# Two quads of heads in the same strips of PSUM, and a new order of the steps in a slot, in a fused attention and mixture-of-experts layer

## The chip, the core and the metric

The kernel runs on one core of a Trainium2 chip. The metric is the device time of one execution, in microseconds (us). A core has TensorE (PE in the profile; its weight loads are PEld), VectorE (DVE), ScalarE (ACT), GpSimd (POOL) and SyncE (SP), which issues most DMAs. Each works through its own instructions in order, and they wait for one another on semaphores.

## What is computed

One transformer layer over x of 16 batches of 256 rows of 128 numbers, in float32: causal attention with 16 heads of 8 numbers, a projection, two layer norms, and for each row the two best of 14 experts (a 128x256 and a 256x128 layer with gelu), weighed, added and normed again. Cut to what matters:

```
qkv = target @ w_qkv;  q, k, v -> 16 heads of 8
scores = q k^T / sqrt(8), causal;  attn = softmax(scores)
out = attn @ v (heads side by side);  proj = out @ w_proj + b_proj
x = layernorm(target + layernorm(proj + target) * gamma + beta)
logits = x @ gate_w.T;  the two best experts of each row, their softmax weights
x = layernorm(x + clip(x + w0 * expert0(x) + w1 * expert1(x), -100, 100))
```

## The kernel before

There are three stages: attention with the choice of experts (until about 290 us in the profile), the expert tiles (to about 462 us), and the sums with the last layer norm. The change is in the first.

**Slots and units.** Each engine has a body(t, r, lap) that is run for t = 0 to B + 5 (B = 16 batches), unrolled. A slot t brings one new batch in and moves the others one step on: batch t is turned and projected to q, k, v; batch t-2 gets its row maxima; batches t-3 and t-4 their scores, exponentials and values; t-4 its projection, t-5 its norms and its gate, t-6 its row numbers and the scatter of its rows to DRAM. In a slot TensorE, ScalarE and GpSimd go through eight units u = 0 to 7. The order of the steps in the code is the order of the work.

**Row maxima.** maxima(t, r, i) on TensorE (L1485) fills both banks of M with q k^T of two or four pairs of heads, masked (L1506, L1512), for i = 0 to 5 at units 0 to 5. reduce(i) on VectorE (L1194, the instruction is L1202) takes the maxima. maxima(i) waits until reduce(i-1) is done, reduce(i) until maxima(i) are; there is one M. At u = 7 TensorE turns the row maxima (L1609), ScalarE negates them in two steps (L920, L931, with L1688 between), and a DMA puts them into q_stack.

**Scores and values.** scores (L1460) computes one pair of heads into S[n % 2], ScalarE takes the exponential (L862) into probs, and for four of the eight pairs GpSimd masks them (L748). values(t, r, s, k) (L1516) multiplies the four heads of quad k by probs. Each head has 32 columns of v_aug: 8 of values, a one (which gives the sum of the row), 23 zeros. So a head has a strip of 32 partitions of O, and a quad 128. Even quads go to columns 0 to 255 of O, odd ones to 256 to 511. pv_quad (L486) places quads 2 and 3 of batch t-4 at u = 2 and 3, quads 0 and 1 of batch t-3 at u = 5 and 7. ScalarE copies O (128x512) to heads_t at u = 7 (L938) and u = 3 (L896). turn_heads(t, i) (L1536) turns the four 128x128 blocks of one half of the rows into G at u = 4 and u = 5; VectorE divides them by the sums (invert_sums, L1211, and normalise_heads, L1217) into heads, which are turned again at u = 6 (L1712) and multiplied by wproj at u = 7 (L1681).

**What else stands in a slot of TensorE.** u = 1: the ranks (L1645) and the turn of x (L1550). u = 2: project (L1558). u = 4: the v projection into O (L1672), copied to v_aug by ScalarE (L899). u = 6: the turn of x2 (L1707), which waits for all six reductions, since it writes to M. u = 7: the gate (L1615), which waits for ScalarE's copy of that (x2T, L912). In each unit the order is: scores; at u = 7 the turn of the row maxima, then the gate; project; rank; turn of x; maxima; turn_heads(0) and the v projection; turn_heads(1); at u = 7 the projection of the heads and the second part of the shift; values; turn of x2 and of the heads.

**What else stands in a slot of VectorE.** From the first reduction on: means and variances (L1247), row_chosen (L1251), reduce(1), yg, row_no (L1234), reduce(2), ys, the split of q and k (rest, L1034), reduce(3), the statistics of ys, reduce(4), invert_sums(0), normalise_heads(0), reduce(5), the same for 1, then the search for the best experts (L1315, L1318), which waits for the gate, chosen (L1320), y (L1327), and the statistics of y (L1227). maxima(0) of the next slot wait for chosen, as its logits lie in M.

**GpSimd** issues the scatter of batch t-6 in four indirect DMAs (L775) at u = 2 to 5, once row_no is there.

## Time and profile before

| | us |
|---|---|
| median of 3 runs | 504.61 (498.4 to 506.06) |
| the profiled execution, its time | 504.69 |
| the profiled execution, its span | 502.9 |
| TensorE, VectorE busy | 379.2, 325.1 |
| ScalarE, GpSimd busy | 266.8, 290.3 |
| mean granted TensorE clock | 0.886 of 2.4 GHz |

The span goes from the first to the last instruction. The slots of the attention stage are counted from the first row-maximum reduction of one (reduce(0)) to that of the next. Slot 5 begins at 64.71 us, slot 7 at 95.82, slot 12 at 182.76, slot 13 at 198.93, slot 16 at 251.68. "remote" in a row means that the profile didn't tell whose signal ended the wait.

### The profile page before, as it was taken

How to read it: one execution, taken by the hardware profiler on the slowest of the kernel's cores; microseconds unless marked ns; L12 is line 12 of the kernel's file. 1: busy time of each engine (PE TensorE's matmuls, PEld its weight loads, DVE VectorE, ACT ScalarE, POOL GpSimd, SP SyncE). 2: the span in 40 equal slices, each digit the busy share in tenths (PEclk: the TensorE clock that was granted, in tenths of full speed). 3: DMA queues.
4: the chain of work that ended last, by engine and by line, in shares of the span. 5: the costliest groups of instructions: out<-in, count | busy, mean ns of one | idle time of the engine just before them, and what ended most of it. 6: DMA issues, size and time to landing. Idle time of an engine off the chain costs nothing. (4 is left out here: it accounts for less than half of the span.)

```text
span 502.9 us, 12961 instructions
## 1 busy us (share of the span) xinstructions
PE 379.2 (75%) x4207; PEld 276.0 (55%) x4207; DVE 325.1 (65%) x1053; ACT 266.8 (53%) x624; POOL 290.3 (58%) x454
## 2 busy tenths in 40 slices
PE   5477988977988798879877867765577877777780
PEld 3244555655555555556544435765466867756580
DVE  6634687758777877786786846734444776663386
ACT  2124666756776577666645637443346544444054
POOL 6402346775777668666754365785554555556271
PEclk9556999989999899998989869978787989798996
DMA  5412333334334433442311141222332222220573
GB/s 137 106 52 65 85 101 98 103 87 110 101 91 107 110 84 90 118 113 66 89 50 55 42 68 28 64 69 63 94 108 67 70 69 75 71 69 21 169 230 105
DMA packets 72974, 44.02 MB, mean 88 GB/s; under 512 B 13233, under 2 KB 68931, under 8 KB 72796
## 3 DMA queue, kind: packets, MB, share of 16 engines
q1 hardware_dynamic: 66650, 33.11, 25.0%
q0 software_dynamic: 4640, 9.36, 5.7%
q10 hardware_dynamic: 1618, 0.73, 0.6%
q8 instruction: 34, 0.56, 0.5%
q14 instruction: 32, 0.26, 0.2%
HBM read 18.54 MB, written 12.36 MB: 61 GB/s over the span
## 5 line engine op out<-in xcount | busy, mean ns | idle before, releaser
L1202 DVE TENSOR_REDUCE row_max<-M 128x4 f32<-128x1024 f32 (+1 forms) x96 | 117.2, 1221 | 48.8 <-PE M L1512 37.3
L862 ACT ACTIVATE probs<-S 128x768 f32<-128x768 f32 x128 | 102.7, 816 | 58.3 <-PE S L1481 42.5
L729 POOL DMA_INDIRECT results<-tile_rows x77 | 77.2, 1002 | 57.0 <-DVE tile_rows L1074 37.4
L775 POOL DMA_INDIRECT sorted_rows<-x,row_no x64 | 65.7, 1027 | 33.5 <-DVE row_no L1234 21.0
L1506 PE MATMUL M<-k_stack,q_stack 64*128 64x128 bf16 (+1 forms) x512 | 41.7, 267 | 43.4 <-DVE row_max L1202 40.3
L1531 PE MATMUL O<-probs,diag 128*32 128x256 f32 (+1 forms) x1024 | 58.5, 349 | 3.1 <-DVE row_chosen L1251 3.1
L748 POOL TENSOR_SCALAR_AFFINE_SELECT probs<-probs 128x256 f32<-128x256 f32 x104 | 40.0, 409 | 23.3 <-ACT probs L862 23.2
L1506 PEld LDWEIGHTS M<-k_stack,q_stack 64*128 64x128 bf16 x512 | 16.7, 100 | 62.6 <-DVE row_max L1202 57.0
L1473 PE MATMUL S<-q_stack,k_stack 64*128 64x256 bf16 (+1 forms) x512 | 45.6, 260 | 0.0
L1531 PEld LDWEIGHTS O<-probs,diag 128*32 128x32 f32 x1024 | 27.7, 113 | 25.4 <-issue 9.3
L852 ACT ACTIVATE hT<-S,q_stack 128x128 f32<-128x128 f32 x78 | 25.7, 371 | 25.0 <-PE S L1577 16.0
L782 POOL TENSOR_TENSOR diag<-rest,diag 128x512 bf16<-128x512 f32 x16 | 18.5, 1155 | 35.5 <-ACT diag L882 24.7
L852 ACT ACTIVATE hT<-S,k_stack 128x128 f32<-128x128 f32 x76 | 24.8, 371 | 20.5 <-PE S L1577 9.7
L1577 PE MATMUL S<-rows_t,k_stack 128*128 128x128 f32 x152 | 28.3, 318 | 7.7 <-ACT hT L852 4.4
L1512 PE MATMUL M<-ident_fold,mask_m 64*128 64x128 bf16 (+1 forms) x384 | 33.1, 255 | 0.0
L1577 PE MATMUL S<-rows_t,q_stack 128*128 128x128 f32 x156 | 27.1, 301 | 4.4 <-issue 2.7
L1577 PEld LDWEIGHTS S<-rows_t,k_stack 128*128 128x128 f32 x152 | 24.7, 231 | 8.9 <-issue 8.9
L1584 PE MATMUL M<-k_stack,hT 128*128 128x128 f32 x132 | 24.5, 317 | 4.1 <-DVE tile_rows L1074 3.5
L1473 PEld LDWEIGHTS S<-q_stack,k_stack 64*128 64x128 bf16 x512 | 16.6, 97 | 19.4 <-issue 17.1
L1065 DVE COPY q_stack<-experts 128x642 f32 x39 | 21.7, 559 | 8.0 <-issue 5.0
L1577 PEld LDWEIGHTS S<-rows_t,q_stack 128*128 128x128 f32 x156 | 23.4, 215 | 5.4 <-issue 5.3
L1584 PE MATMUL M<-q_stack,hT 128*128 128x128 f32 x116 | 21.9, 319 | 5.1 <-DVE tile_rows L1074 5.0
(261 smaller groups left out, 861.5 us busy)
## 6 DMA issues: line engine op xcount, KB each, us to landing
q_stack<-diag SPq DMA_DIRECT2D x96, 64.0 KB
k_stack<-diag SPq DMA_DIRECT2D x85, 64.0 KB
tile_rows<-sorted_rows SPq DMA_DIRECT2D x77, 64.5 KB
experts<-in_L_ffn_w_dram SPq DMA_DIRECT2D x28, 128.0 KB
xin<-in_L_attn_target_dram SPq DMA_DIRECT2D x16, 128.0 KB, 3.0
xres<-in_L_attn_target_dram SPq DMA_DIRECT2D x16, 128.0 KB, 3.1
out_dram<-probs SPq DMA_DIRECT2D x8, 256.0 KB, 2.3
q_stack<-results SPq DMA_DIRECT2D x7, 256.0 KB, 3.2
```

Source lines behind the costliest of these rows:

```text
L729: pool.indirect_dma_start(results, bass.IndirectOffsetOnAxis(ap=y_rows[:, slot, D:ROW].bitcast(U32), axis=0), y_rows[:, slot, 0:D], None, ...
L748: last = pool.affine_select(out=diag, in_=diag, compare_op=ALU.is_ge, fill=0.0, base=0, pattern=[[0, 2], [1, P]], channel_multiplier=-1)
L775: pool.indirect_dma_start(sorted_rows, bass.IndirectOffsetOnAxis(ap=row_no[:, q * 2 * TT + n:q * 2 * TT + n + 1], axis=0), x2[:, q, n % 2, ...
L852: act.activation(hT[:, (s - 2) % HR, f], hidden_of(s - 2, f), ACT.Gelu, bias=expert_now[(s - 2) % XR][:, AT_B1 + f:AT_B1 + f + 1]).then_in ...
L862: act.activation(probs[:, n].rearrange("p (a q) -> p a q", a=2), S[n % 2][:, :].rearrange("p (a q) -> p a q", a=2)[:, :, 0:T + P], ACT.Exp ...
L1202: dve.tensor_reduce(row_max[:, (r - 2) % R, :, g0:g0 + ng, half], M_both[:, :].rearrange("p (a h k) -> p a h k", a=2, h=ng), X, ALU.max).t ...
L1473: last = pe.matmul(S[n % 2][:, 512 * a + at:512 * a + at + nq], k_stack[rows, b, n, half * P:half * P + P], q_stack[rows, b, n, T - nq:T], ...
L1506: pe.matmul(M[a][:, j * keys:j * keys + keys], q_stack[rows, b, g0 + j, half * P:half * P + P], k_stack[rows, b, g0 + j, 0:keys], start=(j ...
L1512: last = pe.matmul(diag, mask_m[rows, c], ident_fold[rows, None, :].broadcast_to([TILE, ng, TILE]), start=False, stop=(c == 1), skip_group ...
L1531: last = pe.matmul(O[32 * j:32 * j + 32, at + T - nq:at + T], v_aug[:, b, half, h], probs[:, h // 2, (h % 2) * (T + P) + of:(h % 2) * (T + ...
L1577: pe.matmul(hidden_of(s - 2, f), expert_now[(s - 2) % XR][:, f * P:f * P + P], rows_t[:, (s - 2) % HR], start=True, stop=True).then_inc(h_ ...
L1584: last = pe.matmul(second(s - 4), hT[:, (s - 4) % HR, f], expert_now[(s - 4) % XR][:, AT_W2 + f * D:AT_W2 + f * D + D], start=(f == 0), st ...
```

## The change

Storage: the four heads of a quad now lie in 4 x 32 columns followed by 16 columns of zeros (v_quads, 144 columns a quad). An odd quad is read 16 columns further left, so its values and sums come out on partitions 16 to 31 of each strip and zeros on 0 to 15. Both quads of a pair are added up in the same 256 columns of O: the even one starts the sum, the odd one ends it. So the copies of O are 128x256, heads_t has two blocks instead of four, turn_heads makes two transposes instead of four, and the heads come out in another order. w_proj's rows are put in that order once, by a matmul with a reordered identity at t = 1, with two copies on VectorE for the identity and one for the result. GpSimd clears the 16 columns in one more memset.

Order on TensorE: maxima stand last in their unit (behind turn_heads, the v projection and values), values stand behind turn_heads(1) and, at u = 7, behind the turn of the row maxima and ahead of the gate, the projection and the second part of the shift. On VectorE invert_sums(0) and normalise_heads(0) stand ahead of reduce(4), and those of 1 ahead of reduce(5).

```diff
+        QUADS = H // 4
+        VQ = 4 * 32 + 16
+        V_SIZE = R * TT * QUADS * VQ
+        v_quads = v_flat.rearrange("p (n c) -> p n c", c=VQ)
+        v_heads = v_quads[:, :, 0:4 * 32].rearrange("p n (j c) -> p n j c", j=4)
...
-        heads_t = sb("heads_t", [P, 4, T])
+        heads_t = sb("heads_t", [P, 2, T])
...
-            sp.dma_start(wproj[:, :], w_proj).then_inc(weights_in, 16)
+            sp.dma_start(wproj_raw, w_proj).then_inc(weights_in, 16)
...
+                pool.memset(v_quads[:, :, 4 * 32:VQ], 0.0).then_inc(consts_p, 1)
...
-                        act.copy(heads_t[:, 2:4], O[:, :].rearrange("p (k q) -> p k q", k=2)).then_inc(o_copied, 1)
+                        act.copy(heads_t[:, 1], O[:, 0:T]).then_inc(o_copied, 1)
...
-                        act.copy(heads_t[:, 0:2], O[:, :].rearrange("p (k q) -> p k q", k=2)).then_inc(o_copied, 1)
+                        act.copy(heads_t[:, 0], O[:, 0:T]).then_inc(o_copied, 1)
...
+            def order_ident():
+                dve.wait_ge(consts, 3)
+                for a in range(2):
+                    part = slice(TILE * a, TILE * a + TILE)
+                    dve.tensor_copy(ident_order[:, part].rearrange("p (j b d) -> p b j d", j=4, b=2),
+                                    ident[:, part].rearrange("p (b j d) -> p b j d", j=4, b=2)).then_inc(ordered, 1)
...
                 dve.wait_ge(gate_turned, 1)
+                dve.tensor_copy(wproj[:, :], M[0][:, P:P + D])
...
-                reduce(4)
                 if on(t - 4):
                     invert_sums(0)
                 if on(t - 4):
                     normalise_heads(0)
+                reduce(4)
                 steps(t, 4)
-                reduce(5)
                 if on(t - 4):
                     invert_sums(1)
                 if on(t - 4):
                     normalise_heads(1)
+                reduce(5)
...
-                at = (k % 2) * T
                 for half, of, nq in ((0, 0, T), (1, T, P)):
                     for j in range(4):
                         h = 4 * k + j
-                        last = pe.matmul(O[32 * j:32 * j + 32, at + T - nq:at + T], v_aug[:, b, half, h],
+                        at = ((b * TT + half) * QUADS + k) * VQ + 32 * j - 16 * (k % 2)
+                        last = pe.matmul(O[32 * j:32 * j + 32, T - nq:T], v_flat[:, at:at + 32],
                                          probs[:, h // 2, (h % 2) * (T + P) + of:(h % 2) * (T + P) + of + nq],
-                                         start=(half == 0), stop=(half == 1), skip_group_check=True)
+                                         start=(half == 0 and k % 2 == 0), stop=(half == 1 and k % 2 == 1), skip_group_check=True)
...
-                for k in range(4):
+                for k in range(2):
                     last = pe.transpose(G[:, k * P:k * P + P], heads_t[:, k, i * P:i * P + P], ident[:, :])
...
+                            pe.wait_ge(ordered, 2)
+                            pe.matmul(M[0][:, P:P + D], ident_order, wproj_raw, start=True, stop=True).then_inc(gate_turned, 1)
...
-                    if u < NM and on(t - 2):
-                        maxima(t, r, u)
...
                     if u == 5 and on(t - 4):
                         pe.wait_ge(o_normed, 2 * (t - 4) + 1)
                         turn_heads(t, 1)
+                    if pv_quad(t, u) and on(pv_quad(t, u)[0]):
...
+                        values(t, r, *pv_quad(t, u))
+                    if u == 7 and on(t - 5):
+                        pe.wait_ge(x2T_copied, t - 4)
...
-                    if pv_quad(t, u) and on(pv_quad(t, u)[0]):
...
-                        values(t, r, *pv_quad(t, u))
...
                         last.then_inc(on_turned, 1)
+                    if u < NM and on(t - 2):
+                        maxima(t, r, u)
```

## Rows read from the trace of the kernel before

**Rows 1.** the page, part 1: each engine, busy us (share of the span), instructions.

```profile
PE 379.2 (75%) x4207; PEld 276.0 (55%) x4207; DVE 325.1 (65%) x1053; ACT 266.8 (53%) x624; POOL 290.3 (58%) x454
```

**Rows 2.** windows (slots, one stretch): PE, PEld, DVE, ACT, POOL busy; PEclk, DMA share, GB/s.

```profile
95.82:114.45 18.63, 15.50 (x213) 10.16 (x211) 12.76 (x35) 11.39 (x24) 12.43 (x23) 0.91 0.33 91
101.30:104.70 3.40, 1.25 (x28) 0.68 (x24) 1.71 (x3) 2.23 (x4) 2.23 (x3) 1.00 0.54 143
164.55:182.76 18.21, 15.50 (x213) 10.17 (x211) 12.76 (x35) 11.53 (x24) 12.27 (x23) 0.91 0.34 94
182.76:198.93 16.17, 14.01 (x213) 9.07 (x210) 12.64 (x36) 11.40 (x24) 11.71 (x21) 1.00 0.39 105
198.93:215.83 16.90, 13.99 (x213) 9.04 (x209) 12.64 (x36) 11.39 (x24) 12.15 (x23) 1.00 0.37 102
215.83:235.33 19.50, 16.68 (x213) 10.80 (x209) 12.75 (x36) 11.48 (x24) 12.60 (x24) 0.82 0.33 88
```

**Rows 3.** the view by lines, VectorE, 95.82 to 251.68 us: xcount | busy, mean ns | idle before.

```profile
L1202 DVE TENSOR_REDUCE row_max<-M 128x4 f32<-128x1024 f32 (+1 forms) x54 | 66.0, 1222 | 21.5 <-PE M L1512 10.6 <-remote 8.4 <-issue 1.3
...
L1315 DVE MAX8 top_v_all<-M 128x8 f32<-128x14 f32 x18 | 2.3, 171 | 16.7 <-PE M L1615 16.7
```

**Rows 4.** the timeline of VectorE, slots 5, 12, 13: start us, us, instruction, [idle before <-releaser].

```profile
70.75 1.21 DVE L1202 TENSOR_REDUCE row_max<-M 128x4 f32<-128x1024 f32 x1
...
189.57 1.23 DVE L1202 TENSOR_REDUCE row_max<-M 128x4 f32<-128x1024 f32 x1 [0.69 <-PE M L1512]
...
198.93 1.22 DVE L1202 TENSOR_REDUCE row_max<-M 128x4 f32<-128x1024 f32 x1 [0.24 <-PE M L1512]
...
200.75 1.23 DVE L1202 TENSOR_REDUCE row_max<-M 128x4 f32<-128x1024 f32 x1 [0.24 <-PE M L1512]
...
202.69 1.22 DVE L1202 TENSOR_REDUCE row_max<-M 128x8 f32<-128x1024 f32 x1
...
206.47 1.23 DVE L1202 TENSOR_REDUCE row_max<-M 128x4 f32<-128x1024 f32 x1 [1.43 <-remote]
...
208.38 1.19 DVE L1202 TENSOR_REDUCE row_max<-M 128x4 f32<-128x1024 f32 x1
209.49 0.25 DVE L1211 RECIPROCAL inv_sum<-G 128x16 f32<-128x16 f32 x1
209.77 0.29 DVE L1217 TENSOR_TENSOR heads<-G,inv_sum 128x128 f32<-128x128 f32 x1
210.29 1.23 DVE L1202 TENSOR_REDUCE row_max<-M 128x8 f32<-128x1024 f32 x1 [0.23 <-PE M L1512]
...
213.71 0.26 DVE L1315 MAX8 top_v_all<-M 128x8 f32<-128x14 f32 x2 [1.71 <-PE M L1615]
...
215.83 1.22 DVE L1202 TENSOR_REDUCE row_max<-M 128x4 f32<-128x1024 f32 x1 [0.24 <-PE M L1512]
```

**Rows 5.** the timeline of TensorE, the slot at 198.93 us.

```profile
202.58 0.86 PE L1531 MATMUL O<-probs,diag 128*32 128x256 f32 x16
203.37 0.34 PE L1473 MATMUL S<-q_stack,k_stack 64*128 64x256 bf16 x4
...
204.41 0.86 PE L1531 MATMUL O<-probs,diag 128*32 128x256 f32 x16
...
207.75 0.39 PE L1506 MATMUL M<-k_stack,q_stack 64*128 64x256 bf16 x4 [2.10 <-DVE row_max L1202]
...
208.18 0.66 PE L1539 MATMUL G<-ident,heads_t 128*128 128x128 f32 x4
...
211.82 0.44 PE L1707 MATMUL M<-ident,x 128*128 128x128 f32 x2
```

**Rows 6.** the timelines of ScalarE and GpSimd, same slot.

```profile
206.63 0.59 ACT L896 COPY heads_t<-O 128x512 f32<-128x512 f32 x1 [0.94 <-PE O L1531]
...
209.32 0.37 ACT L899 COPY diag<-O 128x256 f32<-128x256 f32 x1 [1.40 <-PE O L1672]
...
204.83 0.96 POOL L775 DMA_INDIRECT sorted_rows<-x,row_no  x1 [0.30 <-issue]
```

More of the change, by code:

```diff
@@ L170, in transformer_layer @@
         yg = sb("yg", [P, TT, D])
+        wproj_raw, ident_order = yg[:, 0], yg[:, 1]
         ys = sb("ys", [P, TT, D])
@@ L300, in transformer_layer @@
         folded = sem("folded")
+        ordered = sem("ordered")
         consts_v = sem("consts_v")
@@ L484, in s_unit, with values_of @@
             return (t - 3, u - 2) if u >= 2 else (t - 4, u + NP - 2)
+        def values_of(r):
+            return v_heads[:, r * TT * QUADS:(r + 1) * TT * QUADS, :, 0:HD]
         def pv_quad(t, u):
@@ L707, in more_constants @@
             def more_constants():
-                pool.memset(v_aug[:, :, :, :, HD:32], 0.0).then_inc(consts_p, 1)
+                pool.memset(v_heads[:, :, :, HD:32], 0.0).then_inc(consts_p, 1)
+                pool.memset(v_quads[:, :, 4 * 32:VQ], 0.0).then_inc(consts_p, 1)
                 pool.wait_ge(consts_p, 1)
-                pool.memset(v_aug[:, :, :, :, HD:HD + 1], 1.0).then_inc(consts_p, 1)
+                pool.memset(v_heads[:, :, :, HD:HD + 1], 1.0).then_inc(consts_p, 1)
                 pool.memset(earlier[:, :], 1.0).then_inc(iotas, 1)
@@ L895, in body @@
                         after(act, o_turned, 2 * (t - 4))
-                        act.copy(heads_t[:, 2:4], O[:, :].rearrange("p (k q) -> p k q", k=2)).then_inc(o_copied, 1)
+                        act.copy(heads_t[:, 1], O[:, 0:T]).then_inc(o_copied, 1)
                     if u == 4 and on(t) and not early(t):
                         act.wait_ge(v_ready, t + 1)
-                        act.copy(v_aug[:, r, :, :, 0:HD],
-                                 O[:, 0:T].rearrange("p (i h d) -> p i h d", i=TT, h=H)).then_inc(v_copied, 1)
+                        act.copy(values_of(r), O[:, 0:T].rearrange("p (n j d) -> p n j d", j=4, d=HD)).then_inc(v_copied, 1)
                     if u == 5 and on(t - 5):
@@ L1183, in body @@
                     keep_values(t, r)
+                    order_ident()
                     numbers()
@@ L1611, in body @@
                         last.then_inc(shift_turned, 1)
-                    if u == 7 and on(t - 5):
-                        pe.wait_ge(x2T_copied, t - 4)
-                        for i in range(TT):
-                            last = pe.matmul(M[0][:, T + i * E:T + i * E + E], x2T[:, (r - 5) % R, i * P:i * P + P], gate_t[:, :],
-                                             start=True, stop=True)
-                        last.then_inc(gate_ready, 1)
                     if u == 0 and t == 0:
@@ L1677, in body @@
                         turn_heads(t, 1)
+                    if pv_quad(t, u) and on(pv_quad(t, u)[0]):
+                        if u == 2 and on(t - 6):
+                            pe.wait_ge(rank_read, t - 5)
+                            if t == B + 1:
+                                pe.wait_ge(first_table, 1)
+                        if u == 5 and on(t):
+                            pe.wait_ge(v_copied, t + 1)
+                        values(t, r, *pv_quad(t, u))
+                    if u == 7 and on(t - 5):
+                        pe.wait_ge(x2T_copied, t - 4)
+                        for i in range(TT):
+                            last = pe.matmul(M[0][:, T + i * E:T + i * E + E], x2T[:, (r - 5) % R, i * P:i * P + P], gate_t[:, :],
+                                             start=True, stop=True)
+                        last.then_inc(gate_ready, 1)
                     if u == 7 and on(t - 4):
```

29 lines of the change are left out of this document (11 added, 18 removed).

## The prediction, made before the changed kernel ran

> **What bounds the kernel now.** First the page's line of busy times, then stretches by window, then one slot's timelines on VectorE, TensorE, ScalarE and GpSimd. On the page TensorE has the largest share, 75% of 502.9 us [rows 1], but that is an average over stages. The change acts in the attention stage, whose period is the slot t: sixteen batches go through it, one new per slot, each slot with eight units u. So I read one slot and ask what ends each wait.
>
> VectorE has 12.64 us of work in a slot of 16.17 us and in one of 16.90 us, TensorE 14.0 us [rows 2]. Grouped by line over nine slots (95.82 to 251.68 us), VectorE stands idle 21.5 us ahead of the six row-maximum reductions a slot and 16.7 us ahead of the top-8 search (L1315) that waits for the gate [rows 3]: 2.4 and 1.9 us a slot, and close to nothing elsewhere. So VectorE sets the slot, together with those TensorE steps that it waits for. Both engines share one buffer M: maxima(i) can't begin before reduce(i-1) has ended, and reduce(i) not before maxima(i).
>
> In the slot that starts at 198.93 us the six reductions start at 198.93, 200.75, 202.69, 206.47, 208.38 and 210.29, the search at 213.71, and the next slot's first reduction at 215.83 [rows 4]. The fourth waits 1.43 us, though its maxima were issued before 204.41, where the values behind them start [rows 4, 5]. Their signal arrives late, and so does that of these values: they end at 205.27 by their row, and ScalarE's copy of O (L896), which waits for them, starts at 206.63 [rows 5, 6]. Meanwhile GpSimd issues its scatter of rows twice, close together, the second from 204.83 to 205.79 [rows 6]. The slots before the first scatter don't have this wait: the fourth reduction of slot 5, at 70.75 us, stands without one [rows 4]. I call it the held signal and take its place as tied to the scatters, which hang on the second reduction of the slot; nothing in the change moves them against that.
>
> TensorE's own largest wait in the slot is 2.10 us ahead of maxima(4) at 207.75, for reduce(3) [rows 5].
>
> **The clock.** Three slots are longer than their neighbours: 18.63, 18.21 and 19.50 us, at a mean granted clock of 0.91, 0.91 and 0.82, against 16.17 and 16.90 at 1.00 (mean 16.54) [rows 2]. Together that is 56.34 - 3 x 16.54 = 6.7 us. Ahead of the first of them, in 101.3 to 104.7 us, TensorE was busy 1.25 of 3.40 us, the hold and the wait for reduce(3) in one piece [rows 2]; then it was granted half its clock (1.2 instead of 2.4 GHz).
>
> **The change, part by part**, in the slot at 198.93.
>
> (a) At u = 2 values(t-4,2) now stand ahead of maxima(2). By start to start the values take 203.37 - 202.58 = 0.79 us [rows 5]. VectorE is ready for reduce(2) at 202.69 and had it at once; now maxima(2) end 0.79 later and reduce(2) starts 0.8 us later. VectorE's work behind it (ys, rest) moves along. Bounds: +0.8 if nothing covers it, 0 if TensorE had room, which it hasn't: project ends as maxima(2) begin.
>
> (b) At u = 3 values(t-4,3) stand ahead of maxima(3). VectorE is now ready for reduce(3) 0.8 us later, 205.85 instead of 205.04, but the held signal comes at 206.4 all the same. So 1.43 us of cover hides the 0.8 of (a): net 0 at reduce(3). In two or three slots the wait was shorter (0.69 us at 189.57 [rows 4]) and some of (a) shows: 0.5 us over all. Without a scatter (slots 4, 5) there is no cover, and in slot 6 nearly none: 3 x 0.8 = 2.4 us.
>
> (c) At u = 4 the order on VectorE is now reciprocal and scaling of the first half of the heads, then reduce(4). Between reduce(3) and reduce(4) come 0.28 + 0.29 = 0.57 us (starts at 209.49 and 209.77, 0.29 long [rows 4]). TensorE is ready: turn_heads(0) (0.66 us long with its four transposes [rows 5]) and the v projection, of as many matmuls of that width, now run while reduce(3) runs, as soon as ScalarE has copied O at 206.63 + 0.37 = 207.0, and are done near 208.0. A group of maxima takes 0.6 us from the end of one reduction (200.15) to the start of the next (200.75 [rows 4]), so maxima(4) end near 208.6, before VectorE asks at 208.95. The four transposes of a turn become two, so half of the 0.66, some 0.3 us, goes each time, unseen. reduce(4) comes 1.91 + 0.54 = 2.45 us after reduce(3). Price +0.54; if VectorE were not the bound here it would be between -0.2 and +0.54.
>
> (d) At u = 5 turn_heads(1) and values(t-3,0) (0.79) stand ahead of maxima(5). They fit under reduce(4), which takes 1.2 us; then maxima(5) need 0.6 us and VectorE does its other 0.57 meanwhile. reduce(5) again comes 1.9 us after reduce(4): 0.
>
> (e) From reduce(5) to the search. Before: it ends at 211.51, the turn of x2 (L1707) comes at 211.82, behind values and scores, then scores and the turn of the row maxima, the gate (L1615), and the search at 213.71 [rows 4, 5]. x2 waits for all reductions, so now it starts 0.05 us after the last: -0.26. Then the same steps up to the turn of the row maxima, and there values(t-3,1) come ahead of the gate: +0.79. ScalarE's copy of x2T stands beside these steps before and after, so it gives nothing back. Net +0.53. VectorE has nothing else to do: it waits 2.7 us for the gate instead of 1.71 [rows 4]. Bounds: 0 (if the gate's place were free) and +0.79.
>
> (f) From the search to the next reduce(0): 2.12 us before, of which VectorE works until 215.59 and waits 0.24 for maxima [rows 4]. Now TensorE has less behind the gate and VectorE is the bound: 1.90 us, so -0.22. maxima(0) must also wait for the chosen experts, which come in the middle of this work; by my sum VectorE remains the bound by 0.1.
>
> (g) Less work: the two copies of O have half the elements. They took 0.59 us; a copy of that half size, L899, 0.37 [rows 6]. 0.4 us a slot on ScalarE, 0.6 on TensorE in the transposes. In slots 4 to 17 neither sets the time. In the two slots behind, where no maxima are left and TensorE and ScalarE pace the chain, I take -0.3 each.
>
> (h) Once, at the start: two small copies for the reordered identity, one matmul and one copy for the reordered projection weights, a second memset on GpSimd. Each is no larger than the 0.37 us copy [rows 6] but the memset, which nothing waits for until slot 3. Between 0 (beside other work) and 4 x 0.37 = 1.5 us; I take 0.3, since this stage waits for its loads. The queue of SP gets the same DMAs.
>
> **Sum.** An ordinary slot: 0.54 + 0.53 - 0.22 = +0.85 us. Slots 5 to 17 are thirteen: 11.1. Uncovered (a): 2.4 + 0.5 = 2.9. Together +14.0. Less 0.6 in the tail, plus 0.3 at the start: +13.7. Against it stands the clock: TensorE now works through the hold (turn_heads(0) and v from 207.0), its longest wait falls from 2.1 to about 1.3 us, and the three falls of the clock in this stage should mostly go. I take back 6 of the 6.7 us. Result +7.7 us. The profiled execution took 504.69 us (span 502.9, 1.8 around it), as good as the median of 504.61: 504.7 + 7.7 = 512.4, **512 us**.
>
> A rule of the Trainium skill bears on (b). "SBUF - State Buffer", Who interferes with whom, says that a DMA never contends with a compute engine and that TensorE's ports wait on nobody. By that rule the hold would not come from the scatters and would be part of TensorE's own order; what that gives is the second rival below. The rows speak against the rule only by coincidence in time. On the clock, "TensorE: Matmul & The Clock Gate", Part 1, says that idle stretches bring the half-rate state and sustained work ends it; the rows agree (1.25 busy of 3.40 us ahead of the fall), and it is why I expect some of the falls to go.
>
> **Rivals.**
> 1. *TensorE, not VectorE, is the bound, and in-order waits were its cost: faster.* Place: maxima(4) no longer stop the head's turn and the v projection behind them (2.10 us of waiting, rows 5), and maxima(2), (3), (5) no longer stop values. From the point where reduce(2) starts no later than 1.94 us after reduce(1), each slot gets shorter by what TensorE no longer waits, some 2.10 - 1.3 = 0.8 us, and 0.6 for the transposes that go: at the best 13 x 1.4 = 18, 487 us. VectorE has 12.64 of work in a slot of 16.5 and waits elsewhere, so I halve that: 504.7 - 9 = 496, and with the falls of the clock gone 490. For it: TensorE's 75% share and 14.0 busy us. Against: VectorE waits for the gate already, and the gate moves back.
> 2. *The hold belongs to TensorE's order.* Then it moves back with maxima(3), (a) is covered nowhere, and nine slots pay 0.8 more: +7.2, 520 us.
> 3. *The falls of the clock stay.* 512 + 6 = 518 us. For it: TensorE still waits in this stage, at other places.
> 4. *The gate's place costs nothing*, since ScalarE's copy held it anyway: without (e) 13 x 0.53 = 6.9 less, 505 us, no change.
>
> **Chances.** Forecast 0.42, its own range 507 to 517; rival 1 0.20; rival 2 0.13; rival 3 0.10; rival 4 0.15. The range 494 to 520 leaves out the better half of rival 1 and the top of 2 and 3. A measurement of this kernel can tell about 2% from no change (494.5 and 514.7 us): faster by over 2% 0.18, within 0.50, slower 0.32.
>
> **What would show it.** Right: search 3.95 us behind reduce(5) (3.42 before) with an idle time of 2.7; reduce(2) 2.75 us behind reduce(1); reduce(3) still 7.5 us behind reduce(0); reduce(4) 2.45 behind reduce(3); slots of 17.0 to 17.8 us; clock near 1.00 through 64 to 250 us. Wrong: an idle time ahead of the search near 1.7 (rival 4), a fourth reduction 8.3 us behind the first (rival 2), slots under 16 us (rival 1).

## The result, and the profile after: slower by 5%

The changed kernel took 531.11 us (median of 4 runs, 525.61 to 541.79), the kernel before 504.13 us on the same chip: ratio 1.0536, 95% interval 1.0414 to 1.0657. The forecast of 512 us missed, and so did its range. The ratio leaves out slow executions, that of 541.79 us among them, and the profile of the kernel before is of an execution of 504.69 us, 1.3% above its fastest. The profiled execution took 525.61 us, 20.9 more than that of before.

The page of the changed kernel: part 1, and from part 5 the row-maximum reductions (L1225, before L1202) and the search (L1338, before L1315).

```profile
PE 376.8 (72%) x4145; PEld 276.7 (53%) x4145; DVE 323.0 (62%) x1056; ACT 262.3 (50%) x624; POOL 290.4 (55%) x455
...
L1225 DVE TENSOR_REDUCE row_max<-M 128x4 f32<-128x1024 f32 (+1 forms) x96 | 117.3, 1222 | 58.8 <-PE M L1535 57.5
...
L1338 DVE MAX8 top_v_all<-M 128x8 f32<-128x14 f32 x32 | 4.1, 170 | 45.4 <-PE M L1708 41.8
```

No engine is busy more than 0.7 us longer than before [rows 1]; the time went into waits. The view by lines over the same nine slots as in [rows 3] (7 to 15, now 97.28 to 268.14 us: 170.9 us instead of 155.9) says where:

```profile
L1225 DVE TENSOR_REDUCE row_max<-M 128x4 f32<-128x1024 f32 (+1 forms) x54 | 65.9, 1220 | 29.3 <-PE M L1535 28.2 <-remote 1.0
...
L1338 DVE MAX8 top_v_all<-M 128x8 f32<-128x14 f32 x18 | 2.3, 170 | 24.5 <-PE M L1708 24.5
```

The reductions wait 29.3 us (21.5 before), the search 24.5 (16.7 before): +15.6 in nine slots. The rest of the 20.9: slots 5, 6 and 16 are 1.4, 3.2 and 3.1 us longer, the start 3.2 shorter (reduce(0) of slot 5 at 61.53 us, 64.71 before), and some 1.5 come behind slot 16.

Windows of the changed kernel: the stage, slot 13, the 3.41 us at half clock in it (last row) and as long a stretch ahead of that (columns as in [rows 2]).

```profile
64.00:276.00 212.00, 164.62 (x2301) 107.98 (x2299) 141.75 (x396) 125.32 (x245) 131.37 (x241) 0.90 0.32 88
209.93:228.55 18.62, 14.53 (x210) 9.73 (x205) 12.62 (x36) 11.28 (x24) 12.09 (x22) 0.91 0.34 92
214.75:218.16 3.41, 1.65 (x34) 1.02 (x27) 2.53 (x5) 1.98 (x4) 2.32 (x3) 1.00 0.53 142
218.16:221.57 3.41, 3.41 (x28) 2.20 (x31) 3.17 (x9) 1.86 (x4) 1.98 (x6) 0.50 0.40 101
```

Such a fall now comes in every slot from 6 on, nine between 64 and 250 us, where the kernel before had three stretches at half clock; so has pack_alone below, which keeps that order. The timeline of VectorE in slot 13, reductions and search:

```profile
209.93 1.21 DVE L1225 TENSOR_REDUCE row_max<-M 128x4 f32<-128x1024 f32 x1
...
211.75 1.22 DVE L1225 TENSOR_REDUCE row_max<-M 128x4 f32<-128x1024 f32 x1 [0.25 <-PE M L1535]
...
214.42 1.22 DVE L1225 TENSOR_REDUCE row_max<-M 128x8 f32<-128x1024 f32 x1 [0.81 <-PE M L1535]
...
217.65 1.22 DVE L1225 TENSOR_REDUCE row_max<-M 128x4 f32<-128x1024 f32 x1 [0.88 <-PE M L1535]
...
220.18 1.23 DVE L1225 TENSOR_REDUCE row_max<-M 128x4 f32<-128x1024 f32 x1
...
222.97 1.22 DVE L1225 TENSOR_REDUCE row_max<-M 128x8 f32<-128x1024 f32 x1 [1.08 <-PE M L1535]
226.77 0.26 DVE L1338 MAX8 top_v_all<-M 128x8 f32<-128x14 f32 x2 [2.58 <-PE M L1708]
...
228.55 1.21 DVE L1225 TENSOR_REDUCE row_max<-M 128x4 f32<-128x1024 f32 x1
```

Against [rows 4], step by step: reduce(2) 2.67 us behind reduce(1) (1.94 before), reduce(3) 7.72 behind reduce(0) (7.54), reduce(4) 2.53 (1.91), **reduce(5) 2.79 (1.91)**, search 3.80 (3.42), next reduce(0) 1.78 (2.12). The slot is 18.62 us; eight of the nine take 18.6 to 19.0, slot 15 takes 20.95. The timeline of TensorE shows why reduce(5) is late here:

```profile
216.20 0.28 PE L1504 MATMUL S<-ident_fold,mask_s 64*128 64x128 bf16 x4
217.98 0.55 PE L1562 MATMUL G<-ident,heads_t 128*128 128x128 f32 x2 [1.50 <-ACT heads_t L911]
218.32 1.06 PE L1689 MATMUL O<-wqk_raw,flat 128*128 128x128 f32 x4
...
221.00 1.11 PE L1554 MATMUL O<-probs,flat 128*32 128x256 f32 x16
222.05 0.40 PE L1529 MATMUL M<-k_stack,q_stack 64*128 64x128 bf16 x8
222.28 0.38 PE L1535 MATMUL M<-ident_fold,mask_m 64*128 64x256 bf16 x4
```

TensorE waits 1.50 us for ScalarE's copy of the heads, its clock falls at 218.16, and the v projection (1.06 us; 0.61 at full clock) and the values (1.11; 0.86) push maxima(5) to 222.66. GpSimd issues three of its four scatters between 214 and 222 us:

```profile
214.43 1.09 POOL L790 DMA_INDIRECT sorted_rows<-x,row_no  x1 [1.68 <-DVE row_no L1257]
215.82 0.96 POOL L790 DMA_INDIRECT sorted_rows<-x,row_no  x1 [0.30 <-issue]
...
221.50 1.07 POOL L790 DMA_INDIRECT sorted_rows<-x,row_no  x1 [0.17 <-issue]
```

Which part of the late reduce(5) is TensorE's own, the signals tell. In slots 6, 8, 10, 12 and 14 reduce(5) starts 0.04 us behind the end of maxima(5), so all of the 3.2 to 3.3 us from reduce(4) is TensorE's late work. In slots 7, 9, 11 and 13 it starts 0.3 us behind that end, in slots 15 and 16 1.1 and 0.9: there the signal itself is late too, and the scatter of step 4 (221.50 in slot 13) starts 0.4 to 1.2 us ahead of the end of maxima(5).

### The profile page after: what moved, and what is told of

Same layout as the page of the kernel before. It is cut to its first block and busy times, and to the rows that moved or that the text cites. A ratio compares the mean times of both kernels' runs of the same rounds, so it can differ in the third digit from the quotient of the medians.

```text
span 523.9 us, 12841 instructions
## 1 busy us (share of the span) xinstructions
PE 376.8 (72%) x4145; PEld 276.7 (53%) x4145; DVE 323.0 (62%) x1056; ACT 262.3 (50%) x624; POOL 290.4 (55%) x455
## 5 line engine op out<-in xcount | busy, mean ns | idle before, releaser
L1225 DVE TENSOR_REDUCE row_max<-M 128x4 f32<-128x1024 f32 (+1 forms) x96 | 117.3, 1222 | 58.8 <-PE M L1535 57.5
L1554 PE MATMUL O<-probs,flat 128*32 128x256 f32 (+1 forms) x1024 | 66.7, 372 | 3.0 <-DVE row_chosen L1274 3.0
L1554 PEld LDWEIGHTS O<-probs,flat 128*32 128x32 f32 x1024 | 32.7, 120 | 28.4 <-issue 15.0
L797 POOL TENSOR_TENSOR flat<-rest,flat 128x512 bf16<-128x512 f32 x16 | 18.5, 1154 | 42.2 <-ACT flat L897 24.8
L1562 PE MATMUL G<-ident,heads_t 128*128 128x128 f32 x64 | 17.0, 355 | 22.5 <-ACT heads_t L911 14.3
L1338 DVE MAX8 top_v_all<-M 128x8 f32<-128x14 f32 x32 | 4.1, 170 | 45.4 <-PE M L1708 41.8
L1600 PE MATMUL S<-rows_t,k_stack 128*128 128x128 f32 x152 | 26.8, 304 | 6.5 <-ACT rows_t L861 4.5
L1600 PE MATMUL S<-rows_t,q_stack 128*128 128x128 f32 x156 | 28.5, 313 | 3.7 <-issue 1.8
L1600 PEld LDWEIGHTS S<-rows_t,k_stack 128*128 128x128 f32 x152 | 23.1, 217 | 7.5 <-issue 7.5
L1600 PEld LDWEIGHTS S<-rows_t,q_stack 128*128 128x128 f32 x156 | 24.7, 226 | 4.3 <-issue 4.3
L1607 PEld LDWEIGHTS M<-k_stack,hT 128*128 128x128 f32 x132 | 19.7, 215 | 11.7 <-issue 11.4
```

What stands on the lines that cost most here:

```text
L1225: dve.tensor_reduce(row_max[:, (r - 2) % R, :, g0:g0 + ng, half], M_both[:, :].rearrange("p (a h k) -> p a h k", a=2, h=ng), X, ALU.max).t ...
L1554: last = pe.matmul(O[32 * j:32 * j + 32, T - nq:T], v_flat[:, at:at + 32], probs[:, h // 2, (h % 2) * (T + P) + of:(h % 2) * (T + P) + of ...
L1600: pe.matmul(hidden_of(s - 2, f), expert_now[(s - 2) % XR][:, f * P:f * P + P], rows_t[:, (s - 2) % HR], start=True, stop=True).then_inc(h_ ...
L1607: last = pe.matmul(second(s - 4), hT[:, (s - 4) % HR, f], expert_now[(s - 4) % XR][:, AT_W2 + f * D:AT_W2 + f * D + D], start=(f == 0), st ...
```

## The experiments

All were timed against the kernel before on the same chip; times of different sessions are compared by their ratios. Theory 1 at first: the new order makes TensorE wait in one piece, and its clock falls behind that wait. Its rival: VectorE's own waits are enough. Theory 1 had a second part, from the prediction: TensorE's signals are held back where two scatters stand close together.

**Parts of the change, scatters as they were.** a_warm gives TensorE work in the wait, with two extra 256-column matmuls into G whose result nothing reads:

```diff
                     if u == 4 and on(t - 4) and on(t):
+                        pe.wait_ge(rest_left, t + 1)
+                        for i in range(2):
+                            pe.matmul(G[:, 0:T], ident[:, :], xT[:, r], start=True, stop=True)
```

> The changed kernel with two added float32 matmuls of 128x256 into G at u = 4 (identity by xT), between the split of q and k and the first turn of the heads, in slots 4 to 15; their result is overwritten. They fill a wait of TensorE of 1.5 us with about 1.1 us of work. Theory 1 (the fall of the clock in every slot is a large part of the loss): the falls of the clock between 100 and 250 us become fewer, reduce(5) comes about 1.9 us behind reduce(4) instead of 2.8 to 3.3, slots of about 17.6 us instead of 18.8, in all 8 to 12 us less than the changed kernel (about 519). Theory 2 (the order alone costs it, the clock is a by-product): the same time as the changed kernel within 3 us, or longer by the added work.

Measured: 536.92 us, 1.0762 (1.066 to 1.0863). Six half-clock stretches between 64 and 250 us instead of nine, but longer ones, a mean clock there of 0.89 instead of 0.92, and slots of 20.0 to 20.8 us. Filling that wait did not help; the stretches came elsewhere. It is no clean test, since the added matmuls (1.13 us at full clock) also stand ahead of maxima(4).

a_gate_first puts only the values of step 7 back behind the gate's scores, the projection and the shift:

```diff
-                    if pv_quad(t, u) and on(pv_quad(t, u)[0]):
+                    if u != 7 and pv_quad(t, u) and on(pv_quad(t, u)[0]):
...
                                   start=False, stop=True, skip_group_check=True).then_inc(shift_left, 1)
+                    if u == 7 and on(t - 3):
+                        values(t, r, t - 3, 1)
```

> The changed kernel with one step put back: at u = 7 values(t-3,1) stand behind the gate, the projection and the second part of the shift again. By my step (e) the search then comes 3.1 us behind reduce(5) instead of 3.8, its idle time is 1.8 instead of 2.6, and the piece from the search to reduce(0) is about 2.1 instead of 1.8: 0.4 to 0.5 us a slot less, 5 to 7 us in all. If TensorE's row of work and not VectorE's wait for the gate set the slot, nothing changes within 2 us.

Measured: 529.26 us, 1.0636 (1.0536 to 1.0735). In slot 7 the search stands 3.15 us behind reduce(5) and waits 1.93, so the gate's place costs 0.65 us. The 5 to 7 us in all did not come: in slots 6 and 7 it is given back at half clock, with 3.3 to 3.8 us from the search to the next reduce(0), and in slots 6, 8, 11 and 14 the search itself stands 4.3 to 4.4 us behind reduce(5).

pack_alone keeps the packing and the new numbering of the values, with the order of before on both engines:

```diff
+                    if u < NM and on(t - 2):
+                        maxima(t, r, u)
                     if u == 4 and on(t - 4):
                         pe.wait_ge(o_copied, 2 * (t - 3))
```

> The packing of two quads into the same strips alone: the storage, the smaller copies and the two transposes of the change, with the order of the kernel before on TensorE and VectorE. By my step (g) these save work that sets no time: 504 us within 4. If the packing itself costs something (the odd read, the accumulation over two quads), it comes out slower than 508.

Measured: 502.31 us, 1.0111 (0.9987 to 1.0235): no difference that can be told. The loss is the order's.

a_max_first puts all maxima and VectorE's order back and leaves the values' new place; a_max23_first puts back only maxima(2) and (3):

```diff
+                    if u in (2, 3) and on(t - 2):
+                        maxima(t, r, u)
                     if u == 4 and on(t - 4):
...
-                    if u < NM and on(t - 2):
+                    if u < NM and u not in (2, 3) and on(t - 2):
                         maxima(t, r, u)
```

> The changed kernel with the maxima put back ahead of the slot's other work at every step, and VectorE's order put back with them; the values stay where the change put them, behind the turn of the row maxima. Theory 1 (it is the maxima's place that costs, by the waits of VectorE and by the clock): reduce(2) and reduce(4) come 1.9 us behind the one ahead again, the half-clock stretch is not in every slot, only the search stands 3.8 instead of 3.4 us behind reduce(5), and the time is 504 to 510, some 22 to 26 us less than after. Rival (it is the values' place): 522 or more.

Measured: 509.33 us, 1.0065 (1.0021 to 1.0109), within the 504 to 510 of theory 1. So most of the loss lies in the maxima's place. Seven falls are left between 64 and 250 us, in slot 7 and in slots 9 to 14.

> The changed kernel with maxima(2) and maxima(3) alone put back ahead of the slot's other work. Theory 1 (the fall of the clock in each slot follows TensorE's wait of 1.5 us ahead of the turn of the heads, which the late signal of values(3) sets, so these maxima do not touch it): reduce(2) 1.9 us behind reduce(1), reduce(3) held until the same moment, the falls stay in every slot, 527 to 532. Rival (the work of steps 2 and 3, done too early or too late, decides whether the clock falls): falls in less than half of the slots, 510 to 518.

Measured: 529.38 us, 1.0523 (1.0448 to 1.0598). So putting maxima(2) and (3) back gains nothing while the signals are held; the late maxima(4) and (5) stay suspected.

**The scatters a step later.** The four scatters of a slot stood at steps 2 to 5; here they stand at 3 to 6, in the changed kernel (a_scatter_later), in the kernel before (b_scatter_later) and with the packing alone (pack_later). The edit, against the changed kernel:

```diff
-            return {3: (0,), 4: (1,), 5: (2,), 6: (3,)}.get(u, ()) if t >= B + 4 else {2: (0,), 3: (1,), 4: (2,), 5: (3,)}.get(u, ())
+            return {3: (0,), 4: (1,), 5: (2,), 6: (3,)}.get(u, ())
```

> The changed kernel with the four scatters of rows one unit later (u = 3 to 6) in all slots, so that GpSimd has the subtraction for the split (L797) and the norm's small steps between the first and the second. If the held signals belong to two scatters close together, reduce(3) no longer waits 0.85 us, TensorE's wait ahead of the turn of the heads gets shorter, the clock falls less often: 10 us less or more (near 515). If the hold belongs to TensorE's order, the fourth reduction still waits 0.85 us, and the time is that of the changed kernel, or longer, since GpSimd is later.

Measured: 512.88 us, 1.0319 (1.0211 to 1.0428), near the 515 that was expected if the held signals belong to the scatters.

> The kernel before, with the four scatters of a slot at steps 3, 4, 5, 6 in every slot instead of at 2, 3, 4, 5 (the last stage does so already). Theory 1 (TensorE's signals are held back while two scatters stand close together, in both orders alike): reduce(3) no longer waits (idle before it 0.5 to 1.7 us before, then near 0), so a slot of full clock takes 15.3 to 15.8 us, and the time falls by 6 to 12 us, to 490 to 496. Rival (the 18 us that later scatters gave the changed kernel came from its order of TensorE's work only): within 2 us of the kernel before.

Measured: 485.15 us, 0.9626 (0.9571 to 0.9681), with no fall of the clock between 64 and 250 us.

> The packing of two quads in the same strips with the order of before on both engines, and the scatters at steps 3 to 6. Theory 1: the two are independent and each engine keeps the order of before, so 488 to 496, faster than both kernels. Rival (packing shortens TensorE's work, and with the hold gone too its clock falls more often): reduce(5) waits 1 us and more in most slots as in the changed kernel, and the time is 500 to 510.

Measured: 485.16 us, 0.961 (0.954 to 0.9681). Both came out below what was expected. Reduce(3) waits 0.08 us at most in slots 6 to 15 of either. So the hold is tied to the scatters, in either order, and a kernel 3.8% faster than before lies one step of the scatters away. The window 64 to 250 us shows the clock, in b_scatter_later:

```profile
64.00:250.00 186.00, 163.34 (x2435) 105.19 (x2435) 148.38 (x408) 128.68 (x250) 135.28 (x249) 1.00 0.39 101
```

The same window of pack_later:

```profile
64.00:250.00 186.00, 160.82 (x2393) 100.58 (x2394) 148.35 (x410) 127.26 (x254) 137.70 (x252) 1.00 0.38 102
```

And of the changed kernel:

```profile
64.00:250.00 186.00, 144.75 (x2034) 95.28 (x2032) 125.86 (x350) 112.94 (x221) 117.11 (x217) 0.92 0.34 91
```

**Which part of the order, with the scatters at 3 to 6.** Same edits as above on a_scatter_later: all maxima first (a_maxfirst_later), maxima(4) and (5) first with VectorE's order back (a_max45_later), maxima(2) and (3) first (a_max23_later). Maxima(0) and (1) stay late in the last two. b_first_alone is the kernel before with its scatters at 2, 4, 5, 6.

> The changed kernel with its scatters at steps 3 to 6, all maxima back ahead of the slot's other work and VectorE's order back; of the new order only the values' place is left. Theory 1 (the values' place costs what it adds ahead of the gate's scores, 0.4 us of waiting before the search less 0.2 to 0.3 us behind it): reduce(5) to the search 3.8 to 4.0 us, no fall of the clock between 64 and 250 us, 487 to 491. Rival (the values' place brings falls by itself, as it had some in nearly every slot while the signals were held): 500 or more.

Measured: 482.88 us, 0.970 (0.957 to 0.9831); one fall, at 240 us.

> The changed kernel with its scatters at steps 3 to 6, maxima(4) and maxima(5) and VectorE's order back, maxima(0) to maxima(3) behind the slot's other work. Theory 1 (the late reduce(2) makes ScalarE's middle part of the split late, the copy of the heads stands behind that on ScalarE, and the turn of the heads makes TensorE wait 1.26 us in one piece, behind which its clock falls): that wait stays, falls stay in at least half of the slots, 500 to 509. Rival (only the sum of VectorE's waits counts, 0.73 us of step 2 and 0.3 us at the search): few falls, 493 to 498.

Measured: 496.81 us, 0.9939 (0.9895 to 0.9983): the rival. From slot 6 to 12 no fall, though TensorE waits as long as ever, now ahead of maxima(4):

```profile
169.79 0.39 PE L1528 MATMUL M<-k_stack,q_stack 64*128 64x256 bf16 x4 [1.47 <-DVE row_max L1224]
```

> The changed kernel with its scatters at steps 3 to 6 and maxima(2) and maxima(3) back ahead of the slot's other work; maxima(4) and maxima(5) stay late, with VectorE's new order. Theory 1: TensorE's wait of 1.26 us ahead of the turn of the heads is gone, falls in at most a quarter of the slots, 0.54 us more of VectorE's time between reduce(3) and reduce(4) and 0.3 us at the search, so 492 to 498. Rival (the late maxima(4) and maxima(5) bring the falls): reduce(5) 2.7 us and more behind reduce(4) in most slots, 504 to 513.

Measured: 507.87 us, 1.0244 (1.0064 to 1.0424): the rival again, and three stretches at half clock between 64 and 250 us. Theory 1 had picked the wrong maxima, and the length of TensorE's one wait as the sign.

> The kernel before with its first scatter at step 2 as it was and the other three at steps 4, 5, 6, so that the first two no longer stand 1.4 us apart. Theory 1 (it takes two scatters close together to hold TensorE's signals back): no wait before reduce(3), 483 to 489, like the kernel with all four a step later. Rival (a scatter at step 2 holds them, whether another follows or not): reduce(3) waits 0.5 to 1.7 us as before, 498 to 506.

Measured: 481.31 us, 0.9659 (0.9476 to 0.9842). Reduce(3) waits 0.03 us at most in slots 7 to 15. The second part of theory 1 had expected that, but it doesn't show that two scatters are needed. In slots 7 to 9 maxima(3) are due 1.04 us behind the one scatter at step 2, and their signal comes 0.34 to 0.54 us late all the same, just in time for VectorE.

**What holds the signal.** The second part of theory 1, two scatters close together, was wrong as well, and a_scatter_later shows it in two slots at full clock. The timeline of GpSimd in slots 9 and 10, the scatter of step 4:

```profile
144.41 1.07 POOL L789 DMA_INDIRECT sorted_rows<-x,row_no  x1 [0.17 <-issue]
...
162.31 1.07 POOL L789 DMA_INDIRECT sorted_rows<-x,row_no  x1 [0.17 <-issue]
```

The timeline of TensorE in the same slots, the end of maxima(5):

```profile
144.50 0.38 PE L1534 MATMUL M<-ident_fold,mask_m 64*128 64x256 bf16 x4
...
162.16 0.38 PE L1534 MATMUL M<-ident_fold,mask_m 64*128 64x256 bf16 x4
```

The timeline of VectorE, reduce(5), which waits for them:

```profile
145.72 1.23 DVE L1224 TENSOR_REDUCE row_max<-M 128x8 f32<-128x1024 f32 x1 [1.03 <-PE M L1534]
...
162.58 1.23 DVE L1224 TENSOR_REDUCE row_max<-M 128x8 f32<-128x1024 f32 x1 [0.23 <-issue]
```

Maxima(5) end 0.47 us behind the scatter's start in slot 9, and reduce(5) starts 0.84 us after that; in slot 10 they end 0.23 us behind it, and reduce(5) starts 0.04 us later. One scatter is enough. A signal is due at the end of the work that sends it. Of the TensorE signals due 0.4 to 1.2 us behind the start of a scatter, 32 of 44 came late in this kernel (80 to 262 us), most of them 1.26 to 1.66 us behind that start; in the changed kernel 25 of 29, those behind the second of two close scatters up to 2.06 us. Of VectorE's and ScalarE's own signals due in the same stretches of the two kernels, none of 69 came even 0.1 us late. Theory 2 is this: each scatter holds back the TensorE signals that are due soon behind its start. The two bounds are those of the count: in the changed kernel maxima(3) are due 0.38 us behind the second scatter and are held too. With the scatters at 3 to 6 it is the scatter of step 4 that catches maxima(5), in ten of the eleven slots 6 to 16; maxima(4) and (5) put first end before it. In b_scatter_later 51 of 56 such signals are late too, but no reduction waits for one directly; the cost is in which signal a scatter catches. It isn't nothing there either: in seven of the nine slots 7 to 15 reduce(2) waits 0.5 us, behind a chain that starts with a held signal. The timeline of all engines in slot 13 of b_scatter_later has it:

```profile
189.10 0.98 POOL L774 DMA_INDIRECT sorted_rows<-x,row_no  x1 [0.17 <-issue]
...
190.71 0.81 ACT L861 ACTIVATE probs<-S 128x768 f32<-128x768 f32 x1 [0.66 <-PE S L1480]
...
191.84 1.13 PE L1557 MATMUL G<-diag,wqk 128*128 128x256 f32 x4 [0.44 <-ACT diag L866]
...
193.56 1.23 DVE L1201 TENSOR_REDUCE row_max<-M 128x8 f32<-128x1024 f32 x1 [0.53 <-PE M L1511]
```

The scores are due at 189.57, 0.47 us behind the scatter, and ScalarE starts on them at 190.71 only. Its copy of the turned x comes behind that, the projection waits 0.44 us for the copy, and maxima(2) come behind the projection.

Theory 2 asked for the scatters at 3, 5, 6, 7 (a_scatter_3567), and for the copy of the heads ahead of the cast on ScalarE, which should take TensorE's wait ahead of the turn away (a_scatter_copy, with the scatters at 3, 5, 6, 7: the block of `heads_t[:, 1]` moved above that of `part_m`). a_max45_first is the changed kernel with maxima(4) and (5) alone put back, scatters as they were.

```diff
-            return {3: (0,), 4: (1,), 5: (2,), 6: (3,)}.get(u, ())
+            return {3: (0,), 5: (1,), 6: (2,), 7: (3,)}.get(u, ())
```

> The changed kernel with its scatters at steps 3, 5, 6, 7. With them at 3 to 6 the scatter of step 4 began 0.46 us ahead of the end of maxima(5), and their signal came 0.8 to 1.1 us late. Theory 2 (each scatter holds back the TensorE signals that fall due 0.4 to 1.3 us behind its start, until 1.3 to 1.7 us behind it): reduce(5) comes 1.9 us behind reduce(4) wherever the clock is full, slots of 16.7 to 16.9 us, and 494 to 501. Rival (the wait before reduce(5) comes from the late maxima and the clock, not from a scatter): reduce(5) 2.7 us and more behind reduce(4) in most slots, 508 to 514.

Measured: 459.94 us, 1.0248 (1.0196 to 1.0301). Reduce(5) comes 1.94 us behind reduce(4) and a slot takes 16.7 us, as theory 2 had it; but this chip took only 448.5 us for the kernel before, and its trace shows few late signals, so that is no test of the theory.

> The one before this (the changed kernel, scatters at 3, 5, 6, 7) with ScalarE's copy of the heads at step 3 ahead of its middle part of the split. If TensorE's wait of 1.26 us ahead of the turn of the heads brings falls of the clock: that wait shrinks below 0.6 us, the falls between 64 and 250 us get fewer, and the time is 4 us or more below the one before this. Rival (this wait lies on no path and brings no falls): within 3 us of it.

Measured: 461.58 us, 1.0272 (1.0226 to 1.0318). The wait is 0.43 us instead of 1.26 and the time is the same; but the run above has no fall to take away, so whether the wait brings falls it can't tell.

> The changed kernel, scatters where they were, with maxima(4) and maxima(5) alone put back ahead of the slot's other work and VectorE's order with them. Theory 2 (most of the loss comes from the late maxima(4) and maxima(5): 0.5 us ahead of reduce(4), and 1 us and more ahead of reduce(5)): reduce(4) and reduce(5) come 1.9 us behind the one ahead in most slots, 508 to 514. Rival (the late maxima(2), through ScalarE's late copy of the heads, brings the falls of the clock): 523 to 530.

Measured: 465.62 us, 1.0363 (1.0293 to 1.0433): neither expectation fits in us, on a chip 55 us quicker. As a ratio the rival's does (523 of 504.1 is 1.037), but there are no held signals here for either to be about. So three kernels ran on one chip once more; it was again one of the quick kind (448.75 us for the kernel before).

> The changed kernel, unaltered, on one chip with the two after it. The chip of the last three ran the kernel before in 448.5 us and showed no held signal of TensorE behind a scatter. Theory 2 (held signals and the falls of the clock that come with them make the loss beyond the sum of 0.85 us in a slot): on a chip with held signals 1.05 to 1.06 of before; on a chip without them reduce(3) waits 0 and reduce(5) comes 1.9 us behind reduce(4), and 1.02 to 1.03 of before. Rival (the order alone brings the loss): 1.05 or more on either.

Measured, the changed kernel unaltered: 463.83 us, **1.0326** (1.0258 to 1.0394), next to the 1.02 to 1.03 that theory 2 had for such a chip. The rival, 1.05 or more by the order alone, is refuted.

> The changed kernel with its scatters at steps 3, 5, 6, 7 once more, since the first chip it ran on showed no held signals and could not tell. On a chip that shows them, theory 2: reduce(5) 1.9 us behind reduce(4) where the clock is full, and 0.985 to 1.005 of before, against 1.03 with them at 3, 4, 5, 6. Rival (not the scatter of step 4 but the late maxima and the clock): 1.02 or more. On a chip without held signals: the same as changed, 1.02 to 1.03.

Measured: 460.36 us, 1.0241 (1.0177 to 1.0305), as expected on a chip without held signals.

> The changed kernel with maxima(4) and maxima(5) put back ahead of the slot's other work, with VectorE's order, once more for the same reason. On a chip that shows held signals, theory 2 (most of the loss comes from the late maxima(4) and (5)): 1.01 to 1.03 of before, 20 us below the changed kernel. Rival (the late maxima(2) brings it): 1.04 or more. On a chip without them: 1.03 to 1.04, as on the last one.

Measured: 466.93 us, 1.0431 (1.0357 to 1.0505), 3 us above the changed kernel.

The changed kernel on the quick chip, windows of the stage and the timeline of VectorE in slot 12, to be held against that of slot 13 above:

```profile
64.00:276.00 212.00, 164.40 (x2586) 111.27 (x2589) 159.21 (x446) 137.65 (x270) 143.44 (x262) 0.99 0.34 93
```

```profile
179.27 1.21 DVE L1225 TENSOR_REDUCE row_max<-M 128x4 f32<-128x1024 f32 x1
...
181.08 1.23 DVE L1225 TENSOR_REDUCE row_max<-M 128x4 f32<-128x1024 f32 x1 [0.24 <-PE M L1535]
...
183.75 1.23 DVE L1225 TENSOR_REDUCE row_max<-M 128x8 f32<-128x1024 f32 x1 [0.80 <-PE M L1535]
...
186.02 1.22 DVE L1225 TENSOR_REDUCE row_max<-M 128x4 f32<-128x1024 f32 x1
...
188.44 1.22 DVE L1225 TENSOR_REDUCE row_max<-M 128x4 f32<-128x1024 f32 x1
...
190.38 1.23 DVE L1225 TENSOR_REDUCE row_max<-M 128x8 f32<-128x1024 f32 x1 [0.22 <-PE M L1535]
194.18 0.26 DVE L1338 MAX8 top_v_all<-M 128x8 f32<-128x14 f32 x2 [2.58 <-PE M L1708]
```

The same program with the same scatters: reduce(3) has no wait, reduce(5) comes 1.94 us behind reduce(4), the clock is full, and the slot is 16.70 us instead of 18.6 to 19.0. Here 8 of 75 signals due in that span behind a scatter were late, and three slots pay 0.3 to 0.5 us more ahead of reduce(5); with the scatters at 3, 5, 6, 7 none does. Slots 7 to 15 take 152.1 us, against 170.9. No trace of the kernel before was taken on a quick chip.

## Why the prediction was wrong, point by point

The slot's own sum was nearly right, and the steps that failed are the credit for the clock and (d). Over slots 6 to 16 the way from reduce(4) to reduce(5) takes 12.2 us more than eleven times 1.94; the profiled execution lies 13.2 us above the +7.7 of the forecast. Measured in the changed kernel on its first chip, and on a quick one:

| step, from start to start | forecast | slot 13 above | quick chip, slot 12 |
|---|---|---|---|
| (a) reduce(1) to reduce(2) | 2.75 | 2.67 | 2.67 |
| (b) reduce(0) to reduce(3) | 7.5 | 7.72 | 6.75, no hold |
| (c) reduce(3) to reduce(4) | 2.45 | 2.53 | 2.42 |
| (d) reduce(4) to reduce(5) | 1.9 | **2.79** | 1.94 |
| (e) reduce(5) to search | 3.95 | 3.80 | 3.80 |
| (f) search to reduce(0) | 1.90 | 1.78 | 1.79 |
| granted clock in the stage | near 1.00 | **0.90** | 0.99 |

- (a), (c), (e), (f) right within 0.15 us, with the idle time of 2.58 us ahead of the search where 2.7 was forecast. a_gate_first confirms (e): 0.65 us for the gate's place.
- (b) right: the held signal covers (a), and rival 2 is refuted. Where there is no hold, (a) is uncovered: an undisturbed slot of b_first_alone takes 15.4 to 15.5 us, one of the changed kernel on the quick chip 16.70, so 1.2 to 1.3 dearer. The forecast had 0.85 covered and 1.65 uncovered; of the difference 0.16 is in (e), 0.10 in (f).
- **(d) failed**: "They fit under reduce(4)" leaves out that they may run at half clock, 2.8 to 3.3 us in every slot from 6 on. It also leaves out the scatter of step 4, which can catch the signal of maxima(5): in ten slots with the scatters moved, and in the changed kernel itself in six, for 0.3 us in four of them and 1.1 and 0.9 us in slots 15 and 16.
- **The clock failed**: "the three falls of the clock in this stage should mostly go" and the 6 us taken back. They became nine, and TensorE's work ahead of maxima(5) ran at half clock. The longest wait did shrink, from 2.10 [rows 5] to 1.50 us, but it is no measure: TensorE was busy 1.65 of 3.41 us ahead of the fall at 218.16, and fell; 1.25 of 3.40 [rows 2] was only one case; a_max45_later waits 1.47 us in each slot and stays at full clock for seven of them. Rival 3 named the right thing at too small a price: 6 us, where the result lies 19 above the forecast.
- (g) right: the packing sets no time (pack_alone). (h) not seen: the start got 3.2 us shorter. The clock rose at 37 instead of 47 us, which is not the change's doing alone: in b_scatter_later it rose at 37 too, and slot 5 began at 62.69 us.
- Rival 1 (TensorE sets the slot, and the change makes it faster) is refuted: it needed reduce(2) 1.94 us behind reduce(1) and slots under 16 us, and got 2.67 and 18.6. Rival 4 (the gate's place is free) is refuted by a_gate_first.

How the 5.4% split: on the quick chips, where few signals are held, the same change costs 3.3%, 15 us, the size of the +13.7 of the sum without the clock's credit (in part by luck: thirteen slots 1.3 us dearer, and a start 3 us shorter, the order of before taken from traces on other chips). The further 2% come with the held signals and the falls, if the kinds of chip differ in nothing else that the change meets; the two are not independent, since moving the scatters took the waits and the falls away together in b_scatter_later. Within the order, with the scatters at 3 to 6, slots 7 to 15 take 141.6 us (pack_later, order of before), 143.3 (values moved), 152.0 (maxima(0) to (3) late as well), 160.2 (instead maxima(0), (1), (4), (5) late) and 169.7 (all late): the late maxima(4) and (5) are the dearest part where signals are held.

That part is not shown for the quick chips: there a_max45_first, which puts them back, has four falls and is no faster than the changed kernel, 1.04 against 1.03. What decides a fall stays open. Not tried on a chip with held signals: the scatters at 3, 5, 6, 7, though the same program on both kinds of chip, and the two slots of a_scatter_later, leave little room for another cause of the late signals. Why one kind of chip holds them and the other hardly does is open as well.

"SBUF — State Buffer" of the Trainium skill, Who interferes with whom, says that DMA never contends with a compute engine. The matmuls beside a scatter take their usual time in the rows above, so the rule stands as far as the work goes; what is late is the signal of work done, on which the page says nothing. "TensorE: Matmul & The Clock Gate" of the same skill, Part 1, says that idle stretches bring the half-rate state. The rows agree that a fall follows waiting, but a_max45_later and a_warm show that from the length of a wait, or from filling it, no fall could be foretold here.

## What to carry to other kernels

Before an order is changed, look for signals that arrive late behind a GpSimd scatter (the waiting engine starts 0.4 us and more behind the end of the work that it waits for), and move the scatter first: one step gave 3.8% here on the chips that hold signals, more than either order. Look on more than one chip. Credit a change with clock only after a run shows it: the sum of waits held to 0.15 us in most steps, and the guess on the clock, with the held signal beside it, was off by 19 us in all. Put the work that the bounding engine waits for first (maxima, gate), and take independent work behind it, not the reverse.

## What was not expected of the hardware

- A single scatter issued by GpSimd held back TensorE signals due 0.4 to 1.2 us behind its start, mostly until 1.26 to 1.66 us behind it, and no signals of VectorE or ScalarE (0 of 69), on the chips that took 500 to 505 us for the kernel before (TensorE: 32 of 44, 25 of 29). Two scatters 1.39 us apart held one until 1.8 us behind the second.
- On two other chips the kernel before took 448.5 and 448.75 us; in the changed kernel on the second of them 8 of 75 such signals were late. The two kinds differ by 11% on one kernel, and a ratio measured on one kind does not hold for the other (1.054 and 1.033). In the changed kernel 27.5 of the 62.3 us between their two profiles lie ahead of the last row-maximum reduction (300.9 and 273.4 us); the other 34.8 lie behind it, where no experiment looked.
- With the scatters a step later the stage ran at full clock for 186 us in the order of before (1.00 against 0.96), with no more work for TensorE in a slot.
